# Thirty steps on one core: the update one slot behind tanh, and transposes of two slots in one row

## The reference

```python
def step(h, _):
    h = h + 0.01 * jnp.tanh(h)
    h = h * jax.nn.sigmoid(h)
    h = _layernorm(h, ln_w, ln_b)
    h = jnp.einsum('bsc,dc->bsd', h, W) + b
    return (h, None)
x, _ = jax.lax.scan(step, x, None, length=N_ITERS)     # N_ITERS = 30
```

## Time and profile before

| | |
|---|---|
| time, median of 3 runs | 2090.77 us (2089.68 to 2095.47) |
| profiled execution | 2093.84 us, span 2092.1 us |
| PE busy | 1840.7 us, 88% of the span |
| DVE busy | 1643.1 us, 79% |
| ACT busy | 1347.1 us, 64% |
| POOL busy | 1039.6 us, 50% |
| matmuls of the steps, L2351, three-pass groups | 1320 x 3 |
| update `u`, L2425 | 390 of 678 ns |

### The profile page before, as it was taken

How to read it: one execution, slowest core, us unless ns; L and a number is a source line. 1 busy time by engine, 2 the same in 40 slices (tenths; PEclk the granted TensorE clock), 3 DMA queues, 4 the chain that set the end, 5 groups by cost and what they waited for, 6 DMA issues and landing times. The chain is left out here.

```text
span 2092.1 us, 44618 instructions
## 1 busy us (share of the span) xinstructions
PE 1840.7 (88%) x12898; PEld 1752.7 (84%) x12898; DVE 1643.1 (79%) x4222; ACT 1347.1 (64%) x2744; POOL 1039.6 (50%) x1774
## 2 busy tenths in 40 slices
PE   4667899861999999958999978999999999999998
PEld 2556799761999999957999977999899898989997
DVE  5777677552899999954766657999999898989997
ACT  2233355431666767624665657988989898989895
POOL 5442313343455555533000005777777777777774
PEclk9789999975999999979999989999999999999999
DMA  8654467822787887840766510000000000000001
GB/s 286 220 180 141 125 202 162 160 61 95 231 237 231 235 238 228 235 110 2 258 187 186 173 50 1 2 3 2 2 2 2 2 1 1 0 3 2 3 2 67
DMA packets 101098, 226.47 MB, mean 108 GB/s; under 512 B 21409, under 2 KB 51875, under 8 KB 92460
## 3 DMA queue, kind: packets, MB, share of 16 engines
q1 hardware_dynamic: 86316, 206.33, 32.2%
q0 software_dynamic: 14592, 17.91, 4.4%
HBM read 204.43 MB, written 19.75 MB: 107 GB/s over the span
## 5 line engine op out<-in xcount | busy, mean ns | idle before, releaser
L2351 PE MATMUL ffn_psH<-ffn_w2h,ffn_vTh 128*128 128x256 f32 x1320 | 406.1, 308 | 9.8 <-DVE ffn_vTl L2418 9.8
L2351 PE MATMUL ffn_psH<-ffn_w2h,ffn_vTl 128*128 128x256 f32 x1320 | 374.8, 284 | 0.0
L2351 PE MATMUL ffn_psH<-ffn_w2l,ffn_vTh 128*128 128x256 f32 x1320 | 374.1, 283 | 0.0
L2458 POOL TENSOR_SCALAR ffn_vn<-ffn_vn,ffn_rstd,ffn_shift 128x256 f32<-128x256 f32 x540 | 299.7, 560 | 20.0 <-POOL ffn_shift L2468 0.2
L2425 DVE SCALAR_TENSOR_TENSOR ffn_u<-ffn_th,ffn_psH 128x512 f32<-128x512 f32 x390 | 264.6, 678 | 49.0 <-ACT ffn_th L2378 48.9
L2413 DVE BATCH_NORM_STATS2 ffn_stats<-ffn_vn 128x6 f32<-128x256 f32 x780 | 280.8, 402 | 14.5 <-issue 12.3
L2351 PEld LDWEIGHTS ffn_psH<-ffn_w2h,ffn_vTh 128*128 128x128 f32 x1320 | 252.2, 191 | 33.6 <-DVE ffn_vTl L2418 16.5
L2381 ACT ACTIVATE ffn_vn<-ffn_u 128x512 f32<-128x512 f32 x390 | 254.4, 652 | 13.4 <-DVE ffn_u L2425 13.4
L2351 PEld LDWEIGHTS ffn_psH<-ffn_w2l,ffn_vTh 128*128 128x128 f32 x1320 | 253.4, 192 | 0.0
L2351 PEld LDWEIGHTS ffn_psH<-ffn_w2h,ffn_vTl 128*128 128x128 f32 x1320 | 252.5, 191 | 0.0
L2332 PE MATMUL ffn_psT<-ident,ffn_vn 128*128 128x128 f32 x1560 | 233.9, 273 | 11.9 <-ACT ffn_vTh L2372 11.9
(11 more groups left out here) (245 smaller groups left out, 5221.2 us busy)
## 6 DMA issues: line engine op xcount, KB each, us to landing
g_raw<-in_adjt SPq DMA_DIRECT2D x272, 384.0 KB, 3.7
moe_w1raw<-in_wall SPq DMA_DIRECT2D x33, 1024.0 KB
moe_w2raw<-in_wall SPq DMA_DIRECT2D x33, 1024.0 KB, 5.8
g_raw<-in_adjl SPq DMA_DIRECT2D x27, 256.0 KB, 2.7
moe_b<-in_eb SPq DMA_DIRECT2D x33, 128.0 KB, 4.8
x<-in_x SPq DMA_DIRECT2D x8, 384.0 KB, 6.6
xn_rows<-rt_hn SPq DMA_DIRECT2D x8, 384.0 KB, 4.9
x_rows<-x SPq DMA_DIRECT2D x8, 384.0 KB, 5.3
```

The source lines that it names most:

```text
L2351: last = pe.matmul(psH[w % R][:, q * D:(q + 1) * D], a[:, w % R, q * KD + k, :], b[:, k, :], start=(k == 0 and j == 0), stop=(k == KD - 1 ...
L2458: last = pool.tensor_scalar(vn[:, t, :], vn[:, t, :], rstd[:, s:s + 1], shift[:, s:s + 1], ALU.mult, ALU.add)
```

## The change

All stages from the update on get one slot more of lag: U, SILU, STATS, SHIFT and NORM become 5, 6, 7, 8 and 10. TANH stays at 4, so DVE's update reads a tanh that ACT did one slot earlier in its own list. On PE the transposes of slots m and m + 1 are issued together in every second slot, each behind its own waits, and the matmuls of slot m come after both; in the other slots there are only matmuls. No operation is added or taken away.

```diff
-        LOW, MM, TANH, U, SILU, STATS, SHIFT, NORM = 1, 3, 4, 4, 5, 6, 7, 9
+        LOW, MM, TANH, U, SILU, STATS, SHIFT, NORM = 1, 3, 4, 5, 6, 7, 8, 10
@@ def slot (tensor)
-                if m < END:
-                    gr = m % G
-
-                    pe.wait_ge(vn_done, n - G + 1)
-                    if gr in BY_ACT:
-                        pe.wait_ge(vn2_done, by_act(rounds, m - G))
-                    if m - R >= G:
-
-                        pe.wait_ge(copied, n - R - G + 1)
-                        if split(m - R):
-                            pe.wait_ge(lo_done, lows(rounds, m - R))
-                    for q in range(Q):
-                        for k in range(KD):
-                            last = pe.transpose(psT[m % R][:, q * KD + k, :], vn[:, gr * Q + q, k * P:(k + 1) * P],
-                                                g.ident[:])
-                    last.then_inc(turned, 1)
+                if G <= m < END and (m - G) % 2 == 0:
+                    for w, at in ((m, n), (m + 1, n + 1)):
+                        gr = w % G
+
+                        pe.wait_ge(vn_done, at - G + 1)
+                        if gr in BY_ACT:
+                            pe.wait_ge(vn2_done, by_act(rounds, w - G))
+                        if w - R >= G:
+
+                            pe.wait_ge(copied, at - R - G + 1)
+                            if split(w - R):
+                                pe.wait_ge(lo_done, lows(rounds, w - R))
+                        for q in range(Q):
+                            for k in range(KD):
+                                last = pe.transpose(psT[w % R][:, q * KD + k, :],
+                                                    vn[:, gr * Q + q, k * P:(k + 1) * P], g.ident[:])
+                        last.then_inc(turned, 1)
```

## The result

The changed kernel takes 2072.74 us (median of 7 runs, 2070.51 to 2082.85), against 2090.77 before: 0.9918 of it, 95% interval 0.9901 to 0.9936. 18 us were gained; 15 were forecast. One of the four runs of experiment 8, over which its median of 2038.11 is taken, took 6728.03 us; the other three took 2037.16 to 2038.91.

What follows compares the result with a forecast made beforehand. DVE with its waits for tanh, coming through POOL's shift chain, was taken to set the pace. 3.4 less 2.2 us over 14.4 periods gives 17, less 2 at the ends: 15 us, so 2076 us, own range 2066 to 2086, overall 2054 to 2099.

Steps and rivals of the forecast that it cites:

- Step (1): The later lags give DVE's update a tanh one slot older; all 58 waits go, 3.3 us in 26 slots.
- Step (2): DVE's statistics then wait for silu at three places, 1.0, 0.5 and 0.5: 2.0 us in 26 slots.
- Step (3): Transposes of two slots in one PE row save no change-over: no gain taken, bounds 15 us either way.
- Step (4): The paired row makes PE's transposes wait for normalising fewer slots back, matmuls behind them: 0.2 us lost in 26 slots.
- the sign that I named: PE idle before its transposes, released by POOL's or ACT's normalising, 1 to 2 us in most pairs, nil before.
- Step (6): At the ends of the steps a loss of 2 us (0 to 4); the loop's jump of 2.6 us stays.
- the rhythm: The 26-slot period of the steps, from 52.50 to 51.3 us over 14.4 periods: a gain of 17 us.
- R1: Rival: all waits go and PE's 49.7 us in 26 slots is the floor, 40 us gained, 2051 us; chance 0.10.
- R2: Rival: slower, the paired row holds PE if it needs 1.98 us a slot, not 1.88; 2101 us; chance 0.16.

Runs made afterwards that it cites:

- experiment 8: Only the five new lags, transposes one slot a row, and ACT doing silu ahead of copy and tanh: 2038.11 us, 0.9748 of the kernel before.
- 5: Only the five new lags, transposes one slot a row, and ACT's share of the normalising one slot later: 2052.66 us, 0.9821 of the kernel before.
- 6: Only the five new lags, transposes one slot a row, and POOL writing shift ahead of its normalising: 2045.51 us, 0.9788 of the kernel before.
- Experiment 7: The kernel before, with POOL normalising only the first tile of groups 0, 3, 6, 9 and 12, the second left unnormalised: 2048.72 us, 0.9795.
- experiment 4: The changed kernel with POOL writing shift straight after mr, ahead of its normalising: 2092.77 us, 1.0005 of the kernel before.
- experiment 10: The changed kernel, rows of two slots kept, with ACT doing silu ahead of copy and tanh: 2045.43 us, 0.9779 of the kernel before.
- 11: Only the five new lags, with silu first on ACT and shift ahead of the normalising on POOL: 2041.26 us, 0.9748 of the kernel before.
- experiment 3: The changed kernel with ACT's share of the normalising one slot later in ACT's list: 2111.55 us, 1.0101 of the kernel before.

## Why the prediction was right

Point by point, by its own numbers.

Step (1), right: the update waited 41.9 us and waits nowhere in the stretch now. Step (2), right, and shown: the price of 1.0 + 0.5 + 0.5 is what the lags alone show, site by site, and 5, 6 and 8 remove it in three ways. Experiment 7 does for the old lags what these do for the new: it shows that the update's wait came over POOL. In the changed kernel the same losses come in smaller pieces, because after each short slot DVE already loses 0.2 to 0.3 (0.21 idle at 1557.41, then 0.59 at 1562.08; with 0.09 for each, 0.98 together, the 1.0 foreseen). Step (3), right: 3.75 us for two slots against 3.76, and the rows alone make 1.0009.

Step (4), right in kind, in size too small by half: 0.2 us in 26 slots were put, some 3 us in all, and 51.43 - 51.05 (the lags alone) is 0.4, with 6 us between the medians. Its road was read incompletely. I named only the transposes; the trace shows also 58 waits of ACT's copy for PE's matmuls, since the copy reuses the bank of `vTh` of the group four slots before, whose matmuls stand at lag 3 and so are only one slot old (`act.wait_ge(mm_done, n - R + 1)`). And the sign that I named, PE idle 1 to 2 us in most pairs, was wrong: 12.6 us in 32 waits. PE isn't ahead of POOL any more, so it hardly waits itself; it is late and others wait for it.

Step (6) is the term that was mis-sized: a loss of 2 us at the ends, and "the jump stays". The ends cost nothing that I can tell (0.4 us less before the stretches, 0.6 more after the last `u`). The jumps gave back 4.8 us in all: the 2+2 closing of every second period now has its wait exactly where DVE's list jumps, and DVE is idle once for both:

```profile
1508.25 0.24 DVE L2432 BATCH_NORM_AGGREGATE ffn_mv<-ffn_stats 128x2 f32<-128x6 f32 x2
1510.33 0.75 DVE L2414 BATCH_NORM_STATS2 ffn_stats<-ffn_vn 128x6 f32<-128x256 f32 x2 [1.83 <-issue]
```

So the steps brought 19.6 us by the traces: 14.8 from the rhythm, where 17 were put, and 4.8 from the jumps, where nothing was, and the ends didn't take the 2 that were put. That the sum of 15 came near is in part luck: the rhythm brought less than forecast, and the jumps, which the prediction had at nothing, and the ends more.

The 4.8 us are a mean over unlike stretches. Of the changed kernel's six stretches with a jump one takes 54.72 us and the others 52.6 to 53.2; these five alone give back 1.1 us each, about the wait of 1.0 that the jump hides. The sixth is long because of PE's clock:

```profile
1719.61 0.38 PE L2352 MATMUL ffn_psH<-ffn_w2h,ffn_vTh 128*128 128x256 f32 x1 [1.92 <-issue]
...
1721.32 0.41 PE L2352 MATMUL ffn_psH<-ffn_w2h,ffn_vTh 128*128 128x256 f32 x1
1721.54 0.41 PE L2352 MATMUL ffn_psH<-ffn_w2l,ffn_vTh 128*128 128x256 f32 x1
...
1723.13 0.60 ACT L2373 ACTIVATE ffn_vTh<-ffn_psT 128x512 fp32r<-128x512 f32 x1 [3.62 <-PE ffn_psT L2333]
...
1721.00:1723.00 2.00, 2.00 (x11) 2.00 (x11) 1.92 (x6) 0.00 (x0) 1.76 (x4) 0.50 0.02 4
```

The last row has the columns of the earlier trace rows: the granted clock is 0.50 from 1721 to 1723, the lower of its two levels, 1.2 GHz. PE had stood idle for 1.92 us at the jump just before. Matmuls start 0.21 us apart and not 0.12, the transposes come late, ACT's copy waits 3.62 us for them, and the statistics 1.85 at 1724.77. The other traces agree. The lags alone have such a drop behind three of six jumps, and the stretches of these three take 53.7 to 54.1 us and the others 52.0 to 52.3; experiment 4 has two (56.3 and 56.5 among 54.3 to 54.5); experiments 6, 8, 10 and 11 have none, and no long stretch. The kernel before has two as well (0.50 from 1518 to 1520 is one), so its clock wasn't granted in full throughout the steps, but they cost it nothing: 54.9 among 54.9 to 55.2. This is read from the traces, no run varied the clock, and none shows why it falls behind one jump and not behind the next.

R1 was rated as unlikely and stayed out, but its floor can be had: experiment 8 goes below it, 2038 us against 2051, by an edit that the prediction had passed by. R2's place is real (3 and 4 fall into it); its condition, 1.98 us a slot on PE, isn't met. The Trainium skill, in "TensorE: Matmul & The Clock Gate", step by step of a matmul, has matmuls in program order; experiment 3 agrees: PE's 92 waits for ACT's tile, 38.3 us, lie in front of matmuls that read other groups (where PE waits 0.56 us before 1460.93, the `vTl` that the matmuls behind need had been finished at 1457.77), and the kernel is 39 us slower than the changed one.

Open: why DVE's idle time at a jump is itself shorter with the new lags (1.80 to 2.06 us in the changed kernel, 2.28 to 2.62 before). No run was made for it.

## What to carry to other kernels

In a pipeline of lags, price each order of waits as a chain with its number of slots: its latency against that many slots of the busiest engine, place by place, where the groups differ. The row that says who waited for whom names the last link only; here it said tanh, and it was POOL's second tile, several operations earlier. A lag that opens one chain is worth as much as the next chain leaves, and the next one can often be shortened by the order within an engine's slot (silu first: 29 us beyond the lags alone), while slack taken for another edit (the row of two slots) is paid when anything in front of it moves.

## What the runs showed of the hardware that wasn't expected

At each of the loop's six jumps, in every kernel here, DVE stands idle for 1.8 to 2.6 us ahead of the first instruction of the new pass (1.83 at 1510.33, 1.92 at 1611.08); the profile names no releaser for it, or the silu that the instruction reads. In the kernel before, a jump makes its stretch 2.54 us longer; where another wait falls on it, part of that is saved (1.74 in the changed kernel). PE's idle time at the jumps differs: 2.2 to 2.6 us before, with a wait for ACT or DVE ending it, and at most 1.2 us in experiment 10.

Behind some jumps PE's granted clock fell from 1.00 to 0.50 for some 3.5 us. It cost 1.9 us where PE's transposes were what the others waited for (54.72 against 52.86, the mean of the other five), and nothing in the kernel before, where the update's wait set the pace. Eight transposes in a row take 1.03 us and four 0.60: 0.107 to 0.11 each, so merging saves no time on PE.
